# A CIN recommender tower: chunk 1's stores moved to SyncE's queue ahead of the layer-1 loads, and one more layer-2 group split late

## The chip, the cores and the metric

One core of one Trainium2 chip. The metric is device time in microseconds, from launch to end, of one execution; lower is better. Comparisons between kernels are of executions on the same chip.

## The reference

512 samples, 39 fields, embeddings of 16 numbers. Three layers of pairwise products (a compressed interaction network) and a small dense top, all in fp32:

```python
e = stack([tbl_f[ids[:, f]] for f in range(39)], axis=1)   # 512 x 39 x 16
x0 = xk = e
for idx, (W, b) in enumerate(params):                       # three layers, 128 outputs each
    z = relu(einsum('bhd,bkd,hks->bsd', x0, xk, W) + b)
    xk, direct_part = z[:, :64], z[:, 64:]                  # last layer: all of z is direct
logit = sum(concat(direct), axis=-1)                        # over d
h = relu(concat([logit, dense_ctx]) @ W_top1 + b_top1)
h = relu(h @ W_top2 + b_top2)
y = h @ W_top3
```

## The kernel before

The batch goes in NCH = 16 chunks of 32 samples; a chunk is N = 512 columns (sample, d). Layer 0 (L0) has 4 groups of products, layers 1 and 2 (L1, L2) have 10 each. A group is one VectorE multiplication (`prod`, 128x1024) whose two 512-column tiles TensorE then multiplies by weights and adds up in a PSUM bank `z`.

A group is summed in one of two ways. Whole: two fp32 matmuls, which the profile shows as four records. Split: ScalarE rounds the product to fp32r (`high`), GpSimd subtracts to get the rest (`low`), and TensorE runs six fp32r matmuls: high by high weights, high by low weights, low by high weights. `SPLIT` lists the split groups; four of them, in `THROUGH_PSUM`, go tile by tile through the bank `base`, with VectorE making the low half. `high` and `low` have HRING = 4 slots, `prod` has RING = 8.

`stages_of(i)` writes out the order: in step i come L0 of chunk i, the first 6 groups of L2 of chunk i-1 (4 in step 15), L1 of chunk i, the rest of L2 of chunk i-1. Every engine walks that list in order and waits on semaphores. The splits, the slots and the numbers waited for are all counted from it.

The inputs of a chunk: GpSimd gathers 10 tiles of table rows (`gat`, chunks 0 and 1 at the start); two copies of them are stored in DRAM (`x0_rows`, 2 x 1191 rows of 64 bytes, in four DMAs); one DRAM-to-DRAM DMA repeats them five times; then come `x0base` (three DMAs of 78 KB), `spread0` (the L0 factor, 1792 KB) and `spread` in three pieces (the L1 and L2 factor: 768, 768 and 1024 KB, groups 0 to 2, 3 to 5, 6 to 9). SyncE's queue issues all that, except in the start-up, where ScalarE issues some: the second copy of chunk 0, and for chunk 1 all stores (`store_x0(1, (0, 1))`), the repeat (`repeat_second`), and `x0base` and `spread0` (`load_second`). On ScalarE the stores and the repeat of chunk 1 stand after L0 of chunk 0 and before `shared_copies(0, x1, z0, ...)`, the relu copies that make the L1 factor `x1`; `load_second` stands behind those.

SyncE's queue at the start runs: weights, store and loads of chunk 0, `repeat_x0(0)`, the three L1 pieces of chunk 0, those of chunk 1, `store_x0(2)`, then the loop for the chunks after that. What is stored, repeated and loaded is the same in every chunk; in the start-up only the issuing queue and the order differ.

Of the kernel before, what the change touches and what calls it, by code (L numbers as in the profile page):

```python
# [8 lines left out]
P = 128  # L9
B = 512  # L10
F = 39
D = 16
S = 128
# [5 lines left out]
N = CB * D  # L19
# [24 lines left out]
RELU0_AFTER = (3, 3, 3)  # L44
PIECES = ((0, 3), (3, 6), (6, 10))
SPLIT = {"L0": (1,), "L2": (0, 1, 2, 5, 6, 8), "L1": (1, 2, 3, 5, 6, 7, 9)}
THROUGH_PSUM = (("L2", 2), ("L1", 2), ("L1", 6), ("L2", 6))
BASE_AFTER = ("L2", 9)
FIRST_GATHERS = {("L0", 1): 7, ("L1", 2): 1, ("L1", 5): 1, ("L1", 9): 1}
# [28 lines left out]
    return out  # L78

def finish_order(kind, gs):

    out = []
    for g in gs:
        if g not in SPLIT[kind]:
            out.append(g)
        if g - 1 in gs and g - 1 in SPLIT[kind]:
            out.append(g - 1)
    if gs[-1] in SPLIT[kind]:
        out.append(gs[-1])  # L90
    return out

# [4 lines left out]
DONE = {x: n + 1 for n, x in enumerate((c, kind, g) for c, kind, gs in STAGES for g in finish_order(kind, gs))}  # L97
SPLITS = [x for x in ORDER if x[2] in SPLIT[x[1]]]
# [39 lines left out]
def whole(kind):  # L138
    return [g for g in range(G1) if g not in SPLIT[kind]]

# [9 lines left out]
def tower_kernel(nc, ids, offsets, table, w0a, w0b, w1, w1_split, w2, w2_split, biases, wt1, bt1, wt2, bt2, wt3, ctxT, out):  # L150
    with ExitStack() as ctx:
        def sb(name, shape, dt=F32):
            return ctx.enter_context(nc.sbuf_tensor(name, shape, dt))
# [19 lines left out]
        high_w = {k: sb(f"high_w_{k}", [P, 2 * len(SPLIT[k]), S], F32R) for k in SPLIT}  # L173
        low_w = {k: sb(f"low_w_{k}", [P, 2 * len(SPLIT[k]), S], F32R) for k in SPLIT}
# [34 lines left out]
        h2_sum = (base, x2[:, 0, :])  # L209
        ctx_sum = (x1[:, 0, :], x1[:, 1, :], x2[:, 0, :], x2[:, 1, :])  # L210
        y_sum = (z0[0:1, 0:B // 2], z1[0:1, 0:B // 2])

        def sum_bank(c, kind):
            return z0 if kind == "L2" and c == NCH - 1 else {"L0": z0, "L1": z1, "L2": z2}[kind]
# [47 lines left out]
        def _(sp):  # L262
# [78 lines left out]
            for n, (at, end) in enumerate(FIRST_CUTS):  # L341
                load_first(at, end, spread0_first[n], (0, 1))
            repeat_x0(0)
            for p in range(len(PIECES)):
                load_spread(0, p)
            for p in range(len(PIECES)):
                load_spread(1, p)
            store_x0(2)
# [57 lines left out]

        @block.scalar
        def _(act):
            def split_weights(kind, rows, w):
                act.activation(high_w[kind][0:rows, :, :].rearrange("p t s -> p (t s)"), w, ACT.Copy  # L410
                               ).then_inc(high_w_ready, 1)

            def store_x0(c, copies):

                act.wait_ge(gathered[c], 16 * GAT)
                for n in copies:
                    first = x0_dram[c, n * F:n * F + 1, 0:1]
                    act.dma_start(bass.AP(first.tensor, first.offset, [[D, P], [FPT * N, GAT - 1], [1, D]]),
                                  gat[:, c, 0:GAT - 1, :]).then_inc(x0_stored[c], 16)
                    at = n * F + FPT * (GAT - 1)  # L420
                    tail = x0_dram[c, at:at + 1, 0:1]
                    act.dma_start(bass.AP(tail.tensor, tail.offset, [[D, LAST], [1, D]]),
                                  gat[0:LAST, c, GAT - 1, :]).then_inc(x0_stored[c], 16)

            def repeat_second():

# [7 lines left out]
            def load_second():  # L434

                for j in range(DPT):
                    row = x0_dram[1, (F - j * T0) % F:(F - j * T0) % F + 1, 0:1]
                    act.dma_start(x0base[j * F:(j + 1) * F, :], bass.AP(row.tensor, row.offset, [[N, F], [1, N]])
                                  ).then_inc(base_in, 16)
                act.wait_ge(prod_done, PROD_NUMBER[0, "L0", G0 - 1])  # L440
                act.wait_ge(x0_copied[1], 16)
                row = x0_dram[1, 0:1, 0:1]
                act.dma_start(spread0[:, :, :].rearrange("p t n -> p (t n)"),
                              bass.AP(row.tensor, row.offset, [[N, P], [1, T0 * N]])).then_inc(spread0_in, 16)

            def load_first():

# [101 lines left out]
            split_weights("L1", P, w1_part)  # L549
            act.wait_ge(w2_in, 32)  # L550
            split_weights("L2", P, w2_part)
            act.wait_ge(bias_in, 16)
            store_x0(0, (1,))
            load_first()
            take_base(0)
            for i in range(NCH + 1):
                if i == NCH:
                    shared_copies(i - 1, x2, z1, "L1", 1, x2_ready)
                    relu1(i - 1, 2)
                elif i >= 2:  # L560
                    for part in range(3):
                        relu1(i - 1, part)
                for c, kind, gs in stages_of(i):
                    for g in gs:
                        if (c, kind, g) in POOL_NUMBER:
                            take_high(c, kind, g)
                        if (c, kind, g) in TILED_NUMBER:
                            take_tile_high(c, kind, g, 0)
                        if tiled_behind(c, kind, g, 1):
                            take_tile_high(*tiled_behind(c, kind, g, 1), 1)  # L570
                        if i == 1 and kind == "L0" and g == 1:
                            shared_copies(0, x2, z1, "L1", 1, x2_ready)
                            relu1(0, 2)
                        if kind == "L0" and g == G0 - 1 and i >= 2:
                            relu2(i - 2)
                        if i == NCH and g == 2:
                            relu2(i - 2)
                        if kind == "L2" and i < NCH:
                            for part in range(3):
                                if g == RELU0_AFTER[part]:  # L580
                                    relu0(i, part)
                        if (kind, g) == BASE_AFTER and i + 1 < NCH and i >= 1:
                            take_base(i + 1)
                        if i == 0 and (kind, g) == ("L1", G1 - 1):
                            take_base(1)
                    if kind == "L0" and i == 0:
                        store_x0(1, (0, 1))
                        repeat_second()
                        shared_copies(0, x1, z0, "L0", 0, x1_ready)
                        relu0(i, 2)  # L590
                        load_second()
            relu2(NCH - 1)

            act.wait_ge(top_in, 16 * 4)
# [12 lines left out]
        def _(dve):  # L607
# [91 lines left out]
            def split_weights(kind, rows, w, done):  # L699

                dve.wait_ge(high_w_ready, done)
                dve.tensor_tensor(low_w[kind][0:rows, :, :].rearrange("p t s -> p (t s)"), w,
                                  high_w[kind][0:rows, :, :].rearrange("p t s -> p (t s)").bitcast(F32),
                                  ALU.subtract).then_inc(low_w_ready, 1)

            dve.wait_ge(w0_in, 32)
# [7 lines left out]
            dve.wait_ge(gathered[0], 16 * GAT)  # L714
            split_weights("L1", P, w1_part, 2)
            split_weights("L2", P, w2_part, 3)
            for i in range(NCH + 1):
                if i == NCH:
                    shared_copies(i - 1, x2, z1, "L1", 1, x2_ready)
# [28 lines left out]
        def _(pe):  # L748
# [11 lines left out]
            def sum_high(c, kind, g):  # L760

                z = sum_bank(c, kind)
                at = 2 * SPLIT[kind].index(g)
# [12 lines left out]
            def sum_low(c, kind, g, closes):  # L776

                z = sum_bank(c, kind)
                at = 2 * SPLIT[kind].index(g)
# [12 lines left out]
            def sum_stage(c, kind, gs):  # L792

                closing = stage_end(c, kind)
                if kind == "L2" and c == NCH - 1 and gs[0] == 0:
                    pe.wait_ge(r0_ready, NCH)
                elif gs[0] == 0 and c >= 1:
                    pe.wait_ge({"L0": r0_ready, "L1": r1_ready, "L2": r2_ready}[kind], c)
                for g in gs:
                    if g in SPLIT[kind]:  # L800
# [3 lines left out]
                    if g - 1 in gs and g - 1 in SPLIT[kind]:  # L804
                        sum_low(c, kind, g - 1, DONE[c, kind, g - 1] == closing)
                if gs[-1] in SPLIT[kind]:
                    sum_low(c, kind, gs[-1], DONE[c, kind, gs[-1]] == closing)

            pe.wait_ge(ctx_in, 16 * 3)
# [2 lines left out]
                          start=True, stop=True).then_inc(ctx_done, 1)  # L812
            pe.wait_ge(w1_in, 32)
            pe.wait_ge(w2_in, 32)
            pe.wait_ge(low_w_ready, 3)
            for i in range(NCH):
                for c, kind, gs in stages_of(i):
                    sum_stage(c, kind, gs)
# [95 lines left out]
```

## Time and profile before

| | |
|---|---|
| median of 3 runs | 661.51 us (660.06, 661.51, 1059.06) |
| the profiled execution | 660.79 us |
| its span, first to last instruction | 658.8 us |
| TensorE busy | 610.5 us (93%) |
| VectorE busy | 558.9 us (85%) |
| GpSimd busy | 536.6 us (81%) |
| ScalarE busy | 408.2 us (62%) |
| bytes moved | 90.29 MB, mean 137 GB/s |
| mean granted TensorE clock | 0.987 of full |

About 2 us lie outside the span. Of the three runs one is a far outlier; the other two and the profiled one lie within 1.5 us.

### The profile page before, as it was taken

The numbers are of one execution on the slowest core, as the hardware profiler recorded it, in microseconds if no ns is written. First come the engines' busy times: TensorE is split into PE (matmuls) and PEld (weight loads), VectorE is DVE, ScalarE is ACT, GpSimd is POOL, SyncE is SP. The second block draws the span as 40 slices with busy tenths as digits, with TensorE's granted clock in tenths as the row PEclk, the third lists the DMA queues.
The fourth block names the chain that finished last, engine by engine and source line by source line (L and its number), as shares of the span: only waits on it lengthen the run. The fifth ranks groups of instructions, "written<-read, shape, count | busy, mean of one in ns | idle before, by whom it ended". The sixth has DMA issues, their size and how long they took to land. (4 is left out here: it accounts for less than half of the span.)

```text
span 658.8 us, 6297 instructions
## 1 busy us (share of the span) xinstructions
PE 610.5 (93%) x2000; PEld 375.5 (57%) x2000; DVE 558.9 (85%) x632; ACT 408.2 (62%) x550; POOL 536.6 (81%) x325
## 2 busy tenths in 40 slices
PE   4137989999999999999999999999999999999998
PEld 1014546666666665666656665656666566665553
DVE  2327889898989989898989899898989898988971
ACT  2005576667585867766675857676676758575632
POOL 6755889898989989898989999898989896865540
PEclk9976999999999999999999999999999999999999
DMA  6678473655556584736464564737364645620000
GB/s 224 155 173 253 109 210 67 187 120 136 143 122 203 139 250 76 240 77 206 96 182 101 138 187 90 235 77 237 78 200 96 180 110 128 193 64 1 0 0 0
DMA packets 64043, 90.29 MB, mean 137 GB/s; under 512 B 46624, under 2 KB 49568, under 8 KB 60042
## 3 DMA queue, kind: packets, MB, share of 16 engines
q1 hardware_dynamic: 54334, 85.25, 47.1%
q0 software_dynamic: 5120, 1.29, 2.1%
q10 hardware_dynamic: 4556, 3.35, 1.8%
q8 instruction: 15, 0.25, 0.2%
q14 instruction: 18, 0.15, 0.1%
HBM read 87.31 MB, written 8.95 MB: 146 GB/s over the span
## 5 line engine op out<-in xcount | busy, mean ns | idle before, releaser
L385 POOL TENSOR_TENSOR low<-prod,high 128x1024 fp32r<-128x1024 f32 (+1 forms) x160 | 381.0, 2399 | 63.1 <-ACT high L474 60.3
L648 DVE TENSOR_TENSOR prod<-spread,x 128x1024 f32<-128x1024 f32 x256 | 308.1, 1214 | 42.1 <-issue 15.8
L756 PE MATMUL z<-prod,w_sb 128*128 128x512 f32 (+2 forms) x608 | 290.7, 598 | 30.3 <-DVE prod L648 15.4
L474 ACT ACTIVATE high<-prod 128x1024 fp32r<-128x1024 f32 (+1 forms) x160 | 167.9, 1058 | 119.6 <-DVE prod L648 98.0
L773 PE MATMUL z<-high,high_w_L 128*128 128x512 f32 (+1 forms) x448 | 203.0, 453 | 4.4 <-ACT high L484 2.6
L788 PE MATMUL z<-low,high_w_L 128*128 128x512 f32 (+1 forms) x448 | 181.9, 487 | 3.9 <-POOL low L385 2.4
L375 POOL DMA_INDIRECT gat<-table_dram,index x160 | 154.9, 968 | 36.5 <-issue 34.2
L756 PEld LDWEIGHTS z<-prod,w_sb 128*128 128x128 f32 (+2 forms) x608 | 115.8, 191 | 117.0 <-issue 86.6
L773 PE MATMUL z<-high,low_w_L 128*128 128x512 f32 (+1 forms) x448 | 177.9, 397 | 0.0
L788 PEld LDWEIGHTS z<-low,high_w_L 128*128 128x128 f32 (+1 forms) x448 | 82.1, 189 | 69.8 <-issue 45.7
L494 ACT ACTIVATE x<-z,bias_sb 64x512 f32<-64x512 f32 (+1 forms) x174 | 112.5, 646 | 14.0 <-PE z L756 7.4
L484 ACT ACTIVATE high<-base 128x512 fp32r<-128x512 f32 x128 | 75.5, 590 | 56.1 <-DVE base L688 55.6
L773 PEld LDWEIGHTS z<-high,high_w_L 128*128 128x128 f32 (+1 forms) x448 | 84.8, 189 | 42.4 <-issue 14.5
L773 PEld LDWEIGHTS z<-high,low_w_L 128*128 128x128 f32 (+1 forms) x448 | 84.8, 189 | 31.7 <-issue 14.4
L696 DVE TENSOR_TENSOR low<-base,high 128x512 fp32r<-128x512 f32 x128 | 87.8, 686 | 8.6 <-ACT high L484 8.3
L688 DVE TENSOR_TENSOR base<-spread,x 128x512 f32<-128x512 f32 x128 | 88.6, 692 | 2.3
L629 DVE TENSOR_TENSOR prod<-spread,base 117x1024 f32<-117x1024 f32 x64 | 65.4, 1082 | 10.6 <-DMA spread<-x_rows 6.9
L507 ACT ACTIVATE x<-z,bias_sb 32x512 f32<-32x512 f32 x12 | 7.7, 642 | 17.7 <-DMA x_rows<-gat 16.7
L544 ACT ACTIVATE r<-z,bias_sb 128x512 f32<-128x512 f32 x16 | 11.0, 687 | 10.5 <-PE z L788 10.4
L465 ACT ACTIVATE base<-x0base 117x512 f32<-117x512 f32 x16 | 9.6, 602 | 8.8 <-DMA x0base<-x_rows 8.4
L674 DVE TENSOR_REDUCE logit<-r 128x32 f32<-128x512 f32 x16 | 10.9, 678 | 4.8 <-ACT r L544 4.8
L811 PE MATMUL x<-ctx_sb,wt1c_sb 16*128 16x512 f32 x8 | 7.2, 1076 | 7.8 <-DMA bt_sb<-bt_dram 7.8
(37 smaller groups left out, 89.2 us busy)
## 6 DMA issues: line engine op xcount, KB each, us to landing
spread<-x_rows SPq DMA_DIRECT2D x14, 1792.0 KB
spread<-x_rows SPq DMA_DIRECT2D x32, 768.0 KB, 13.3
spread<-x_rows SPq DMA_DIRECT2D x16, 1024.0 KB
x_rows<-x_rows SPq DMA_DIRECT2D x15, 390.0 KB
x0base<-x_rows SPq DMA_DIRECT2D x44, 78.0 KB
gat<-table_dram,index POOLq DMA_INDIRECT x160
x_rows<-gat SPq DMA_DIRECT2D x29, 72.0 KB
spread<-x_rows ACTq DMA_DIRECT2D x1, 1792.0 KB
```

The source lines that it names most:

```text
L375: pool.indirect_dma_start(out=gat[0:rows, c % GBUF, j, :], out_offset=None, in_=table, in_offset=bass.IndirectOffsetOnAxis(ap=index[0:rows ...
L385: pool.tensor_tensor(low[0:rows, h, 0:k, :], prod[0:rows, slot(c, kind, g), 0:k, :], high[0:rows, h, 0:k, :].bitcast(F32), ALU.subtract).t ...
L474: act.activation(high[0:rows, split_slot(c, kind, g), 0:k, :], prod[0:rows, slot(c, kind, g), 0:k, :], ACT.Copy).then_inc(high_ready, 1)
L484: act.activation(high[0:rows, split_slot(c, kind, g), t, :], base[0:rows, :], ACT.Copy).then_inc(tile_high, 1)
L494: act.activation(to[at:end, tile, :], z[k:k + end - at, :], ACT.Relu, bias=bias_sb[k:k + end - at, layer:layer + 1]).then_inc(ready, 1)
L629: dve.tensor_tensor(prod[0:rows, slot(c, "L0", g), 0:k, :], spread0[0:rows, 2 * g:2 * g + k, :], base[0:rows, :].unsqueeze(1).to_broadcast ...
L648: dve.tensor_tensor(prod[0:rows, slot(c, kind, g), :, :], spread[0:rows, c % 2, g, :].unsqueeze(1).to_broadcast([rows, k, N]), x[0:rows, : ...
L688: dve.tensor_tensor(base[0:rows, :], spread[0:rows, c % 2, g, :], x[0:rows, t, :], ALU.mult).then_inc(tile_prod, 1)
L696: dve.tensor_tensor(low[0:rows, h, t, :], base[0:rows, :], high[0:rows, h, t, :].bitcast(F32), ALU.subtract).then_inc(tile_low, 1)
L756: last = pe.matmul(z[:, :], w[0:rows, at + j, :], prod[0:rows, slot(c, kind, g), j, :], start=g == 0 and j == 0, stop=closes and j == k - 1)
L773: pe.matmul(z[:, :], v[kind][0:rows, at + j, :], high[0:rows, h, j, :], start=g == 0 and j == 0 and v is high_w, stop=False)
L788: last = pe.matmul(z[:, :], high_w[kind][0:rows, at + j, :], low[0:rows, h, j, :], start=False, stop=closes and j == k - 1)
```

## The change

`store_again` is the second copy of chunk 0, two DMAs, as before. Start-up: chunk 1's four stores go from ScalarE's queue to SyncE's, right behind `repeat_x0(0)` and ahead of chunk 0's three L1 pieces. Chunk 1's `x0base` and `spread0` loads also go to SyncE's queue, between chunk 0's L1 pieces and chunk 1's. The repeat stays on ScalarE's queue, but now stands behind the relu copies, not ahead of them. Steady state: in the last three chunks group 7 of L2 is split (it was whole); its weights are split once at the start, by one more ScalarE and one more VectorE instruction of 128x256.

```diff
+LATE_SPLIT = {"L0": (), "L2": (7,), "L1": ()}
+LATE_FROM = {"L0": NCH, "L2": NCH - 3, "L1": NCH}
+def split_of(c, kind):
+    return tuple(sorted(SPLIT[kind] + (LATE_SPLIT[kind] if c >= LATE_FROM[kind] else ())))
...
@@ SyncE
             repeat_x0(0)
+            store_x0(1)
             for p in range(len(PIECES)):
                 load_spread(0, p)
+            load_base(1)
+            load_spread0(1)
             for p in range(len(PIECES)):
                 load_spread(1, p)
...
@@ ScalarE
-            def store_x0(c, copies):
+            def store_again():
+                act.wait_ge(gathered[0], 16 * GAT)
...
             split_weights("L2", P, w2_part)
+            split_weights("L2", P, late_part("L2", w2_sb), True)
             act.wait_ge(bias_in, 16)
-            store_x0(0, (1,))
+            store_again()
...
                     if kind == "L0" and i == 0:
-                        store_x0(1, (0, 1))
-                        repeat_second()
                         shared_copies(0, x1, z0, "L0", 0, x1_ready)
                         relu0(i, 2)
-                        load_second()
+                        repeat_second()
...
@@ VectorE
             split_weights("L2", P, w2_part, 3)
+            split_weights("L2", P, late_part("L2", w2_sb), 4, True)
...
@@ TensorE
-            pe.wait_ge(low_w_ready, 3)
+            pe.wait_ge(low_w_ready, 4)
```

`load_base(1)` waits for chunk 1's stores and for `base_ready` 1; `load_spread0(1)` waits for chunk 0's last L0 product and for the repeat; each piece of chunk 1 waits for the repeat.

## Rows read from the trace of the kernel before

**Rows 1.** Windows: busy time of each engine in a stretch of the steady state, clock, DMA share, GB/s
```profile
120.00:160.00 40.00, 39.87 (x138) 25.43 (x137) 35.56 (x41) 28.65 (x40) 36.23 (x24) 1.00 0.54 145
```
**Rows 2.** Timeline of VectorE in the first 70 us: start, duration, instruction, idle before
```profile
38.74 3.13 DVE L662 TENSOR_SCALAR x<-z,bias_sb 32x512 f32<-32x512 f32 x4 [4.42 <-PE z L756]
52.79 2.35 DVE L648 TENSOR_TENSOR prod<-spread,x 128x1024 f32<-128x1024 f32 x2 [10.92 <-ACT x L507]
...
64.15 1.22 DVE L648 TENSOR_TENSOR prod<-spread,x 128x1024 f32<-128x1024 f32 x1
...
68.84 4.08 DVE L629 TENSOR_TENSOR prod<-spread,base 117x1024 f32<-117x1024 f32 x4 [1.75 <-ACT base L465]
```
**Rows 3.** Waits: who waited for whom, us, times, longest
```profile
ACT x L507 <- DMA x_rows<-gat: 16.7, 1, 16.7
```
**Rows 4.** Timeline of ScalarE and of the DMAs it issues (ACTq)
```profile
34.05 0.39 ACTq L418 DMA_DIRECT2D x_rows<-gat  x1
...
36.05 6.22 ACTq L422 DMA_DIRECT2D x_rows<-gat  x1
49.16 0.90 ACTq L430 DMA_DIRECT2D x_rows<-x_rows  x1
50.11 0.64 ACT L507 ACTIVATE x<-z,bias_sb 32x512 f32<-32x512 f32 x1 [16.75 <-DMA x_rows<-gat]
50.25 0.83 ACTq L438 DMA_DIRECT2D x0base<-x_rows  x2
...
53.14 0.37 ACTq L443 DMA_DIRECT2D spread<-x_rows  x1
```
**Rows 5.** Timeline of all engines: VectorE's weight splits, and gathers on GpSimd
```profile
17.89 3.69 DVE L702 TENSOR_TENSOR low_w_L<-spread,high_w_L 128x1792 fp32r<-128x1792 f32 x2 [2.10 <-DMA gat<-table_dram,index]
17.95 2.79 POOL L375 DMA_INDIRECT gat<-table_dram,index  x1 [0.30 <-issue]
...
30.22 0.92 POOL L375 DMA_INDIRECT gat<-table_dram,index  x1 [0.30 <-issue]
```
**Rows 6.** Timeline: SyncE's DMA issues (SPq), and the ScalarE copy that waited for one
```profile
21.47 0.74 SPq L293 DMA_DIRECT2D x0base<-x_rows  x2
...
24.12 0.60 ACT L465 ACTIVATE base<-x0base 117x512 f32<-117x512 f32 x1 [8.42 <-DMA x0base<-x_rows]
...
25.41 0.92 SPq L282 DMA_DIRECT2D x_rows<-x_rows  x1
...
33.69 21.32 SPq L324 DMA_DIRECT2D spread<-x_rows  x6
...
81.43 0.36 SPq L308 DMA_DIRECT2D spread<-x_rows  x1
...
115.22 0.39 SPq L271 DMA_DIRECT2D x_rows<-gat  x1
...
116.76 0.60 SPq L274 DMA_DIRECT2D x_rows<-gat  x1
120.55 0.83 SPq L282 DMA_DIRECT2D x_rows<-x_rows  x1
```
**Rows 7.** Windows of 2 us: engines as in rows 1, clock, DMA share, GB/s
```profile
42.00:44.00 2.00, 0.00 (x0) 0.00 (x0) 0.00 (x0) 0.00 (x0) 1.46 (x2) 0.59 1.08 232
...
84.00:86.00 2.00, 2.00 (x7) 0.99 (x6) 1.10 (x1) 1.92 (x4) 1.39 (x3) 1.00 0.91 380
```
**Rows 8.** The chain that ended last: start, duration, what
```profile
629.77 1.72 PE z L756 x4
...
638.18 0.93 PE z L773 x4
```
**Rows 9.** The costliest groups: busy us, mean ns of one, idle before them
```profile
L385 POOL TENSOR_TENSOR low<-prod,high 128x1024 fp32r<-128x1024 f32 (+1 forms) x160 | 381.0, 2399 | 63.1 <-ACT high L474 60.3
```
**Rows 10.** Timeline of VectorE and TensorE in the last 65 us
```profile
595.43 1.22 DVE L648 TENSOR_TENSOR prod<-spread,x 128x1024 f32<-128x1024 f32 x1 [4.61 <-ACT x L494]
...
628.57 0.51 PE L773 MATMUL z<-high,high_w_L 128*128 128x512 f32 x1 [0.76 <-ACT high L484]
```

More of the change, by code:

```diff
@@ L78, in stages_of, with finish_order @@
     return out
-def finish_order(kind, gs):
+def split_of(c, kind):
+    return tuple(sorted(SPLIT[kind] + (LATE_SPLIT[kind] if c >= LATE_FROM[kind] else ())))
+def finish_order(c, kind, gs):
     out = []
+    split = split_of(c, kind)
     for g in gs:
-        if g not in SPLIT[kind]:
+        if g not in split:
             out.append(g)
-        if g - 1 in gs and g - 1 in SPLIT[kind]:
+        if g - 1 in gs and g - 1 in split:
             out.append(g - 1)
-    if gs[-1] in SPLIT[kind]:
+    if gs[-1] in split:
         out.append(gs[-1])
@@ L96 @@
 NUMBER = {x: n + 1 for n, x in enumerate(ORDER)}
-DONE = {x: n + 1 for n, x in enumerate((c, kind, g) for c, kind, gs in STAGES for g in finish_order(kind, gs))}
-SPLITS = [x for x in ORDER if x[2] in SPLIT[x[1]]]
+DONE = {x: n + 1 for n, x in enumerate((c, kind, g) for c, kind, gs in STAGES for g in finish_order(c, kind, gs))}
+SPLITS = [x for x in ORDER if x[2] in split_of(x[0], x[1])]
 SPLIT_NUMBER = {x: n + 1 for n, x in enumerate(SPLITS)}
@@ L172, in tower_kernel @@
         w2_sb = sb("w2_sb", [P, 2 * len(whole("L2")), S])
-        high_w = {k: sb(f"high_w_{k}", [P, 2 * len(SPLIT[k]), S], F32R) for k in SPLIT}
-        low_w = {k: sb(f"low_w_{k}", [P, 2 * len(SPLIT[k]), S], F32R) for k in SPLIT}
+        high_w = {k: sb(f"high_w_{k}", [P, 2 * len(SPLIT[k] + LATE_SPLIT[k]), S], F32R) for k in SPLIT}
+        low_w = {k: sb(f"low_w_{k}", [P, 2 * len(SPLIT[k] + LATE_SPLIT[k]), S], F32R) for k in SPLIT}
         wide1, wide2 = 2 * len(SPLIT["L1"]) * S, 2 * len(SPLIT["L2"]) * S
@@ L211, in tower_kernel, with split_weight_tiles, late_part @@
         y_sum = (z0[0:1, 0:B // 2], z1[0:1, 0:B // 2])
+        def split_weight_tiles(kind, late):
+            n = 2 * len(SPLIT[kind])
+            return (n, n + 2 * len(LATE_SPLIT[kind])) if late else (0, n)
+        def late_part(kind, w):
+            at = 2 * whole(kind).index(LATE_SPLIT[kind][0])
+            return w[:, at:at + 2, :].rearrange("p t s -> p (t s)")
         def sum_bank(c, kind):
@@ L408, in _, with split_weights @@
         def _(act):
-            def split_weights(kind, rows, w):
-                act.activation(high_w[kind][0:rows, :, :].rearrange("p t s -> p (t s)"), w, ACT.Copy
+            def split_weights(kind, rows, w, late=False):
+                at, end = split_weight_tiles(kind, late)
+                act.activation(high_w[kind][0:rows, at:end, :].rearrange("p t s -> p (t s)"), w, ACT.Copy
                                ).then_inc(high_w_ready, 1)
-            def store_x0(c, copies):
[L415 to L423, printed above, removed]
+            def store_again():
+                act.wait_ge(gathered[0], 16 * GAT)
+                first = x0_dram[0, F:F + 1, 0:1]
+                act.dma_start(bass.AP(first.tensor, first.offset, [[D, P], [FPT * N, GAT - 1], [1, D]]),
+                              gat[:, 0, 0:GAT - 1, :]).then_inc(x0_stored[0], 16)
+                tail = x0_dram[0, F + FPT * (GAT - 1):F + FPT * (GAT - 1) + 1, 0:1]
+                act.dma_start(bass.AP(tail.tensor, tail.offset, [[D, LAST], [1, D]]),
+                              gat[0:LAST, 0, GAT - 1, :]).then_inc(x0_stored[0], 16)
             def repeat_second():
@@ L432, in repeat_second @@
                               ).then_inc(x0_copied[1], 16)
[L434 to L444, printed above, removed]
             def load_first():
@@ L697, in take_tile_low, with split_weights @@
                                   ALU.subtract).then_inc(tile_low, 1)
-            def split_weights(kind, rows, w, done):
+            def split_weights(kind, rows, w, done, late=False):
+                at, end = split_weight_tiles(kind, late)
                 dve.wait_ge(high_w_ready, done)
-                dve.tensor_tensor(low_w[kind][0:rows, :, :].rearrange("p t s -> p (t s)"), w,
-                                  high_w[kind][0:rows, :, :].rearrange("p t s -> p (t s)").bitcast(F32),
+                dve.tensor_tensor(low_w[kind][0:rows, at:end, :].rearrange("p t s -> p (t s)"), w,
+                                  high_w[kind][0:rows, at:end, :].rearrange("p t s -> p (t s)").bitcast(F32),
                                   ALU.subtract).then_inc(low_w_ready, 1)
@@ L778, in sum_low @@
                 z = sum_bank(c, kind)
-                at = 2 * SPLIT[kind].index(g)
+                at = 2 * (SPLIT[kind] + LATE_SPLIT[kind]).index(g)
                 rows, k = shape_of(kind, g)
@@ L799, in sum_stage @@
                 for g in gs:
-                    if g in SPLIT[kind]:
+                    if g in split_of(c, kind):
                         sum_high(c, kind, g)
@@ L803, in sum_stage @@
                         sum_whole(c, kind, g, DONE[c, kind, g] == closing)
-                    if g - 1 in gs and g - 1 in SPLIT[kind]:
+                    if g - 1 in gs and g - 1 in split_of(c, kind):
                         sum_low(c, kind, g - 1, DONE[c, kind, g - 1] == closing)
-                if gs[-1] in SPLIT[kind]:
+                if gs[-1] in split_of(c, kind):
                     sum_low(c, kind, gs[-1], DONE[c, kind, gs[-1]] == closing)
```

2 lines of the change are left out of this document (1 added, 1 removed).

## The prediction

> **What bounds the kernel now.** I read the busy time by stretches first. From about 100 us on TensorE is busy without a gap (39.87 of 40 us, VectorE 35.6, GpSimd 36.2) [rows 1]: only less TensorE work, or an earlier start of this phase, moves the end. The start-up is different. VectorE finishes its four relu copies of chunk 0 at 41.87 (38.74 + 3.13), then idles 10.92 us until the first L1 product at 52.79, and the release is named: ScalarE's half of the same copies [rows 2]. The waits say why ScalarE is late: one wait of 16.7 us for chunk 1's stores [rows 3]. The timeline of ScalarE's queue shows the whole story: it issues the stores at 34.05, one issue takes 6.22 us, the stores have landed at 49.16, and only after the repeat is issued do the copies run from 50.11 [rows 4]. The copies need nothing of chunk 1; it is queue order alone. Meanwhile the DMA engines are full with chunk 0's L1 pieces, which SyncE issued from 33.69 on (2.6 MB, at 232 GB/s in the middle) [rows 6, 7].
>
> From the first L1 product the chain is VectorE's own: L1 takes from 52.79, with group 6 reached at about 64.15, to L0 of chunk 1 at 68.84, 16.05 us later [rows 2]. Whatever the first L1 product gains is kept as long as each load arrives in time for the earlier clock.
>
> **The start-up, part by part.**
>
> ScalarE's copies lose their cover of waits. They start with VectorE's, when L0's last matmul is done (38.7), and take 4 x 0.64 = 2.6 us [rows 2, 4]: done at 41.3. VectorE's, at 41.9, are then the later half. So the copies allow L1 at 41.9.
>
> What is late next is the first L1 piece, since SyncE's queue now issues four stores ahead of it. When can those go? The first store on ScalarE's queue went at 34.05 [rows 4], 2.9 us after the last gather of chunk 1 was issued (30.22 + 0.92) [rows 5]; ScalarE's queue runs ahead of its arithmetic (at 50.25 it issues a load while four activations are still to come [rows 4]), so I take 34.05 as the gathers' landing. One store sequence on SyncE's queue takes 2.14 us to issue (115.22 to 116.76 + 0.60) and 5.33 us until the repeat behind it may go (120.55) [rows 6]. So the first piece is issued at 36.2 instead of 33.69, and the stores have landed at 39.4. The piece is 786 KB: at 232 GB/s 3.4 us, and a small load takes 1.9 us from issue to use (22.21 to 24.12) [rows 6, 7]; 5.3 us, and with the stores' rest in front of it on the same engines up to 6.2. It lands between 41.5 and 42.4. The two terms are near each other; I take 42.2.
>
> One small term on top. VectorE gets one more subtraction of 128x256 right behind the two of 3.69 us. In their shadow a gather took 2.79 us instead of 0.92 [rows 5], so the blocks go together. At 3.69 us for 3328 columns, 256 more are 0.3 to 0.4 us; chunk 1's gathers end that much later, and with them the stores and the piece. The bounds are 0 and 0.4; I take 0.3, because the gather's row shows the effect directly. The Trainium skill ("SBUF — State Buffer", Who interferes with whom) speaks the other way: it infers that tensor_tensor takes only the pair's read side, which does not hold up a gather's descriptors. By that the term would be 0 and the sum 0.3 us better; the row of 2.79 us decides. The same instruction on ScalarE and the raised wait of TensorE (4 instead of 3) end by about 22 us, ahead of the base copy at 24.12 on which every L0 product waits [rows 6]: nothing.
>
> First L1 product: 42.5, against 52.79. Gain 10.3 us. Bounds: 41.9 (gain 10.9) and, if the store issues are as slow as the 6.22 us one, 34.05 + 8.2 + 6.2 = 48.4 (gain 4.4).
>
> Does the rest follow? Group 6 needs the third piece at 42.5 + 11.4 = 53.9. Three pieces of 2.62 MB at 232 GB/s take 11.3 us from about 38: 49.4, plus landing 50.4, plus a share for the repeat: in time. ScalarE issues the repeat now between 39.4 and 42.2, beside these loads. Alone it took 4.0 us (49.16 to 53.14) [rows 4]; chunk 0's, beside other loads, 8.3 (25.41 to 33.69) [rows 6]. So it lands between 43.4 and 50.5; I take 49, as nearest to the crowded row. The wait in front of it holds up ScalarE no longer: the stores (39.4) are in before the copies end. Then SyncE issues `spread0` of chunk 1: 1.84 MB at 380 GB/s are 4.8 us, plus 1.9 [rows 7, 6], with `x0base` ahead: 56 to 57. L0 of chunk 1 wants it at 42.5 + 16.05 = 58.5. It fits by 1.5 us, no more. Chunk 1's L1 pieces, behind it, are in by 69, and wanted at about 76. Cost of these edits: nothing, under that cover; without it, us for us.
>
> TensorE's clock does not come back: it had fallen to 1.2 GHz by 42 to 44 (0.59 in that window) [rows 7], and the first L1 matmul now comes near 43.8, behind the fall. The slow stretch moves along, under VectorE's chain.
>
> **The late split.** A whole group costs TensorE 1.72 us (4 records), a split one six records at 0.93 / 4, 1.40 [rows 8]: 0.32 us less, three times 0.96. It counts only where TensorE sets the end. Chunk 13's (in step 14) does: VectorE later waits 4.61 us for the copies that hang on TensorE's L0 of chunk 15 [rows 10]. From there VectorE leads until TensorE waits last at 628.57 [rows 10]; chunk 14's saving falls in that stretch and is lost. Chunk 15's group 7 comes behind 628.57, on TensorE's chain: kept. So 0.64, upper bound 0.96. The cover: each new split adds a rounding on ScalarE (28.65 of 40 us busy [rows 1]) and a subtraction of 2.4 us on GpSimd [rows 9], which in those steps has no gathers left, ten of 0.92 us [rows 5]. If GpSimd were late all the same, with groups 5, 7 and 8 in a row, TensorE would wait up to 2.4 us once per chunk; on the two chunks that count this is 4.8 against 0.64, the lower bound of -4.2. TensorE takes the low half a group later than the high one, so I stay at 0.64.
>
> **Sum.** 660.8 - 10.3 - 0.6 = 649.9 us, span about 648. The profiled run is 0.7 us below the median of the runs; against that median it is -1.75%. About 2%, 13.2 us, is what a measurement of this kernel can tell from no change as I use the word.
>
> **The rivals.**
>
> Late `spread0`: the repeat crawls, landing at 51 to 54, and L0 of chunk 1 waits 0.5 to 3.5 us. For it: the margin is 1.5 us and the stores' crawl; against: the repeat has only 195 rows of 2 KB. Price 652 (650.5 to 653.5). Chance 0.16.
>
> Stuck issue: SyncE's store issues take what ScalarE's did, the first piece lands at 48.4: 660.8 - 4.4 - 0.6 = 655.8. For it: the one row of 6.22 us; against: SyncE's own row of 2.14. Chance 0.07.
>
> Slower: the pieces flow only when the stores are in, and the stores crawl as they did (15.1 us, to 49.2); the first piece then lands at 49.2 + 6.2 = 55.4, 2.6 us behind 52.79, and the time is 660.8 + 2.6 - 0.6 = 662.8. It decides from stores that land after 46.6. Against it: what made them crawl were the pieces, now behind them. Chance 0.03.
>
> More than the sum: all terms at their good ends (10.9 + 0.96) give 648.9. For the bound of 2% still another us would be needed, such as a first matmul ahead of the clock's fall, or a baseline at the high end of its runs. Chance 0.09, with 647 to 648.5. That the change doesn't do what it says (the split saves nothing) would be 650.5; that it costs its 4.2 us, 654.7; both lie inside the range, the second with a chance of 0.03 taken from the forecast's. The forecast itself, 648.9 to 651.5: 0.62.
>
> Range 647.7 to 655.0: it leaves out the slower case, the stuck issue and half of the best. Faster by over 2%: 0.12; same: 0.84; slower by over 2%: 0.04, for what I have not seen.
>
> **What the new profile would show.** ScalarE's 16.7 us wait gone, its copies beside VectorE's at 38.8; first L1 product at 42 to 43, with a short idle put down to the first piece if my second term holds; L0 of chunk 1 at 58 to 59 without a DMA wait; the phase without gaps about 10 us earlier; TensorE's last wait again on ScalarE in step 16; six records for group 7 in the last chunks. The forecast is wrong if the first product comes after 44, or if VectorE waits for `spread` or ScalarE for `x0base` at chunk 1.

## The result and the profile after

The changed kernel takes 652.12 us in the median of 4 runs (651.20 to 652.47), the kernel before 661.77 on the same chip (661.51 without its outlier of 1059.06 us, which the ratio leaves out): a ratio of 0.9861, 95% interval 0.9837 to 0.9884. The profiled execution took 651.20 us with a span of 649.4, against 660.79 and 658.8. The forecast was 649.9 in a range of 647.7 to 655.0, and "within 2%" was the likeliest class: both hold. The time is 1.3 us (profiled) to 2.2 us (median) above the forecast. The gain is 1.3 us short, 9.6 us against 10.9 us, between the medians as between the profiled executions, since the kernel before has its median above its profiled execution too.

The number alone would not have settled the cause. The median of 652.12 lies outside the 648.9 to 651.5 of "the forecast itself" and inside the 650.5 to 653.5 of the rival with a late `spread0`. The rows decide between the two.

The spans differ by 9.4 us. I follow them by four marks, each a row: first L1 product, first L0 product of chunk 1, first L1 product of chunk 1, TensorE's last wait. VectorE's timeline after, which answers to [rows 2] (78.18 is layer 1 of chunk 1; before it stood at 86.94):

```profile
38.52 3.13 DVE L666 TENSOR_SCALAR x<-z,bias_sb 32x512 f32<-32x512 f32 x4 [3.83 <-PE z L762]
43.70 2.35 DVE L652 TENSOR_TENSOR prod<-spread,x 128x1024 f32<-128x1024 f32 x2 [2.06 <-DMA spread<-x_rows]
...
47.01 1.22 DVE L652 TENSOR_TENSOR prod<-spread,x 128x1024 f32<-128x1024 f32 x1 [0.23 <-DMA spread<-x_rows]
...
60.08 4.08 DVE L633 TENSOR_TENSOR prod<-spread,base 117x1024 f32<-117x1024 f32 x4 [1.75 <-ACT base L470]
...
78.18 2.35 DVE L652 TENSOR_TENSOR prod<-spread,x 128x1024 f32<-128x1024 f32 x2 [1.84 <-ACT x L499]
```

The 10.92 us wait for ScalarE is gone, and a wait of 2.06 us for the first piece stands in its place; then 0.23 us for the second piece. The first L1 product comes 9.09 us earlier than in [rows 2], L0 of chunk 1 8.76 us earlier, layer 1 of chunk 1 8.76 us earlier.

ScalarE and its DMA issues (ACTq) after, against [rows 4]: the copies run beside VectorE's, and the repeat goes at 38.46, since the queue runs ahead of the arithmetic.

```profile
38.44 0.64 ACT L512 ACTIVATE x<-z,bias_sb 32x512 f32<-32x512 f32 x1 [5.26 <-PE z L762]
38.46 0.90 ACTq L447 DMA_DIRECT2D x_rows<-x_rows  x1
39.11 1.98 ACT L512 ACTIVATE x<-z,bias_sb 32x512 f32<-32x512 f32 x3
```

SyncE's issues (SPq) after, against [rows 6]:

```profile
34.57 0.39 SPq L286 DMA_DIRECT2D x_rows<-gat  x1
...
36.75 1.91 SPq L339 DMA_DIRECT2D spread<-x_rows  x3
38.78 1.41 SPq L308 DMA_DIRECT2D x0base<-x_rows  x3
51.77 0.35 SPq L323 DMA_DIRECT2D spread<-x_rows  x1
```

The four stores take 2.18 us of issue, the first piece goes at 36.75, and `spread0` of chunk 1 at 51.77, when the repeat has landed.

The chain that ended last, after, answers to [rows 8, 10]: TensorE waits last at 619.42 (628.57 before), and group 7 of chunk 15 is now in the run of eight records at 0.23 us each.

```profile
619.42 0.73 PE z L779 x2
...
625.94 1.86 PE z L779 x8
```

So: 9.09 at the first product, 0.33 lost by group 3's later start (3.31 us behind the first product instead of 2.99), 8.76 kept over chunk 1, 0.39 gained until the last wait (9.15), 0.25 behind it (649.4 - 619.42 = 29.98, before 658.8 - 628.57 = 30.23). Sum 9.4. The first two experiments ask how much of the 0.39 is the split's.

### The profile page after: what moved, and what is told of

Its sections match the earlier page's. It is cut to its first block and busy times, and to the rows that moved or that the text cites. A ratio compares the mean times of both kernels' runs of the same rounds, so it can differ in the third digit from the quotient of the medians.

```text
span 649.4 us, 6321 instructions
## 1 busy us (share of the span) xinstructions
PE 607.9 (94%) x2006; PEld 375.3 (58%) x2006; DVE 559.2 (86%) x633; ACT 411.6 (63%) x554; POOL 543.3 (84%) x328
## 5 line engine op out<-in xcount | busy, mean ns | idle before, releaser
L403 POOL TENSOR_TENSOR low<-prod,high 128x1024 fp32r<-128x1024 f32 (+1 forms) x163 | 388.0, 2398 | 47.3 <-ACT high L479 46.0
L762 PE MATMUL z<-prod,w_sb 128*128 128x512 f32 (+2 forms) x596 | 284.6, 598 | 22.1 <-DVE prod L633 15.5
L479 ACT ACTIVATE high<-prod 128x1024 fp32r<-128x1024 f32 (+1 forms) x163 | 171.1, 1058 | 123.4 <-DVE prod L652 102.9
L393 POOL DMA_INDIRECT gat<-table_dram,index x160 | 154.6, 966 | 36.5 <-issue 33.8
L762 PEld LDWEIGHTS z<-prod,w_sb 128*128 128x128 f32 (+2 forms) x596 | 113.3, 190 | 107.0 <-issue 85.8
L489 ACT ACTIVATE high<-base 128x512 fp32r<-128x512 f32 x128 | 75.5, 590 | 51.7 <-DVE base L692 51.2
L666 DVE TENSOR_SCALAR x<-z,bias_sb 32x512 f32<-32x512 f32 x12 | 9.1, 757 | 4.2 <-PE z L762 3.8
```

The lines of the kernel that those rows point to most:

```text
L393: pool.indirect_dma_start(out=gat[0:rows, c % GBUF, j, :], out_offset=None, in_=table, in_offset=bass.IndirectOffsetOnAxis(ap=index[0:rows ...
L403: pool.tensor_tensor(low[0:rows, h, 0:k, :], prod[0:rows, slot(c, kind, g), 0:k, :], high[0:rows, h, 0:k, :].bitcast(F32), ALU.subtract).t ...
L479: act.activation(high[0:rows, split_slot(c, kind, g), 0:k, :], prod[0:rows, slot(c, kind, g), 0:k, :], ACT.Copy).then_inc(high_ready, 1)
L489: act.activation(high[0:rows, split_slot(c, kind, g), t, :], base[0:rows, :], ACT.Copy).then_inc(tile_high, 1)
L762: last = pe.matmul(z[:, :], w[0:rows, at + j, :], prod[0:rows, slot(c, kind, g), j, :], start=g == 0 and j == 0, stop=closes and j == k - 1)
```

## The experiments

Each is told by the same marks. Unless a diff says otherwise, it is against the changed kernel.

**Without the late split.**

```diff
-LATE_FROM = {"L0": NCH, "L2": NCH - 3, "L1": NCH}
+LATE_FROM = {"L0": NCH, "L2": NCH, "L1": NCH}
```

> The changed kernel without the late split (group 7 of layer 2 whole in all chunks; its extra weight split at the start is kept). My theory: the split gave 0.3 us ahead of TensorE's last wait (chunk 13) and 0.3 us behind it (chunk 15), nothing for chunk 14; so this kernel's span is 0.6 us above the changed kernel's, 650.0, about 651.9 us; first L1 product still at 43.7. Rival (all three chunks count): 1.0 us. Rival (the split is absorbed): 0.0 us.

Measured: 652.45 us in the median (651.52 to 654.61), the profiled one 651.52, span 649.7. Its last wait is in the chain at

```profile
619.46 0.74 PE z L779 x2
```

From there to the end 30.24 us, against 29.98 with the split: chunk 15's 0.3 us. At the first L1 product, at layer 1 of chunk 1 and at that wait the two profiles agree within 0.05 us. Chunk 13's share is there all the same, between ScalarE's last two sets of six relu copies: they start at 570.71 and 582.31 without the split, and at 570.96 and 582.26 with it, 11.60 against 11.30 us. The 490 us before took 0.24 us more in the profile with the split, and this hides the share in the total; what caused it is open. This pair alone does not settle 0.3 or 0.6.

**The late split alone, on the start-up of before.** Every start-up edit of the diff is taken back, the split is kept.

> The kernel before with the late split alone (the start-up as before: stores, repeat, x0base and spread0 of chunk 1 on ScalarE's queue). Theory: 0.3 us from chunk 13 (the step from ScalarE's second-to-last layer-1 input copies to its last ones shrinks from 11.6 to 11.3 us) and 0.3 us behind TensorE's last wait: 660.1 us, a ratio of 0.999. Rival: nothing, 660.8 us, with that step still 11.6.

Measured over 10 runs: 660.61 us, ratio 0.9990, interval 0.9980 to 0.9999. Layer 1 of chunk 1 on VectorE, and TensorE's last wait:

```profile
86.18 2.35 DVE L674 TENSOR_TENSOR prod<-spread,x 128x1024 f32<-128x1024 f32 x2 [1.84 <-ACT x L519]
```

```profile
627.50 0.50 PE L801 MATMUL z<-high,high_w_L 128*128 128x512 f32 x1 [0.76 <-ACT high L509]
```

541.32 us lie between them; before it was 628.57 - 86.94 = 541.63. Another 30.0 us to the end, 30.2 before. That is 0.3 and 0.2, the two shares of the forecast. The difference of the medians, 0.67 us, agrees, but its interval (0.1 to 1.3 us) would also hold 0.96, all three chunks. ScalarE's last two sets of six relu copies say where the 0.3 arises, first before, then with the split alone:

```profile
579.79 4.00 ACT L494 ACTIVATE x<-z,bias_sb 64x512 f32<-64x512 f32 x6
591.40 4.00 ACT L494 ACTIVATE x<-z,bias_sb 64x512 f32<-64x512 f32 x6 [0.53 <-PE z L756]
```

```profile
579.05 4.00 ACT L519 ACTIVATE x<-z,bias_sb 64x512 f32<-64x512 f32 x6
590.35 4.00 ACT L519 ACTIVATE x<-z,bias_sb 64x512 f32<-64x512 f32 x6 [0.33 <-PE z L784]
```

11.61 us before, 11.30 with the split: chunk 13's share, as in the pair above. From the last set to TensorE's last wait it takes 37.17 us before, 37.15 with the split alone, 37.15 in the changed kernel without the split and 37.16 with it: chunk 14's saving is lost.

**The repeat ahead of ScalarE's copies.**

```diff
+                        repeat_second()
                         shared_copies(0, x1, z0, "L0", 0, x1_ready)
                         relu0(i, 2)
-                        repeat_second()
```

> The changed kernel, but ScalarE waits for the stores and issues the repeat ahead of its relu copies, as before the change. Theory (the gain is the stores on SyncE's queue, ahead of the pieces: they land at 38.2, before L0 ends at 38.5): no change, within 0.3 us of the changed kernel, the repeat issued at about 38.2. Rival (the gain is the order on ScalarE): the copies come late again and several us are lost.

Measured: 651.93 us (651.65 to 652.61). ScalarE, then VectorE:

```profile
37.93 0.90 ACTq L447 DMA_DIRECT2D x_rows<-x_rows  x1
38.89 2.65 ACT L512 ACTIVATE x<-z,bias_sb 32x512 f32<-32x512 f32 x4 [5.62 <-DMA x_rows<-gat]
```

```profile
43.23 2.35 DVE L652 TENSOR_TENSOR prod<-spread,x 128x1024 f32<-128x1024 f32 x2 [2.22 <-DMA spread<-x_rows]
...
59.30 4.08 DVE L633 TENSOR_TENSOR prod<-spread,base 117x1024 f32<-117x1024 f32 x4 [1.75 <-ACT base L470]
```

ScalarE again waits for the stores, but they are in at 37.93, when L0 ends, and nothing is lost. With the stores on SyncE's queue ahead of the pieces the place of the repeat on ScalarE's decides nothing.

**The stores behind the copies on ScalarE's queue.**

```diff
@@ SyncE
-            store_x0(1)
@@ ScalarE
                         relu0(i, 2)
+                        store_second()
                         repeat_second()
```

> The changed kernel, but the four stores stay on ScalarE's queue, behind the relu copies; SyncE loads the pieces of chunk 0 at once. Theory: the copies are done at 41.3 and the first L1 product starts at 41.9, earlier than in the changed kernel, but the stores crawl beside the pieces to about 50, ScalarE stands in the wait of the repeat till then, and VectorE is stopped at the first tile of group 2 (from about 45 to 50); the repeat lands at 54, spread0 of chunk 1 at about 61, L0 of chunk 1 starts at 61 to 63 instead of 60.1: 652.5 to 654.5 us. Rival (order on ScalarE alone makes the gain): 649 to 650 us.

Measured: 656.81 us, ratio 0.9928 (0.9907 to 0.9949). ScalarE, then VectorE:

```profile
43.23 4.78 ACTq L449 DMA_DIRECT2D x_rows<-gat  x1
49.94 0.89 ACTq L457 DMA_DIRECT2D x_rows<-x_rows  x1
50.88 1.06 ACT L489 ACTIVATE high<-prod 128x1024 fp32r<-128x1024 f32 x1 [9.09 <-DMA x_rows<-gat]
```

```profile
41.66 2.35 DVE L663 TENSOR_TENSOR prod<-spread,x 128x1024 f32<-128x1024 f32 x2
...
52.59 0.69 DVE L711 TENSOR_TENSOR low<-base,high 128x512 fp32r<-128x512 f32 x1 [6.73 <-ACT high L499]
...
64.53 4.08 DVE L644 TENSOR_TENSOR prod<-spread,base 117x1024 f32<-117x1024 f32 x4 [1.75 <-ACT base L480]
```

The chain is the one expected: an early start, slow stores (38.44 to 49.94), ScalarE in the wait, VectorE stopped 6.73 us at group 2. So the order on ScalarE's queue alone also gives the early first product. The size was missed: L0 of chunk 1 at 64.5, not 61 to 63, and 656.8 us, not 652.5 to 654.5, since I had not counted the work that group 2's roundings still have ahead of them when ScalarE comes free. The profiled execution also has the fall of the clock that is told further below; it costs 1.2 us behind these rows. The order without the move keeps about half of the gain (0.9928 against 0.9861).

**`x0base` and `spread0` of chunk 1 on ScalarE's queue.**

```diff
@@ SyncE
-            load_base(1)
-            load_spread0(1)
@@ ScalarE
                         repeat_second()
+                        load_second()
```

> The changed kernel with chunk 1's x0base and spread0 loads back on ScalarE's queue, behind the repeat. Theory: ScalarE stands in the wait for the repeat until about 51.7, VectorE is stopped at group 2 of layer 1 (about 46.5 to 53), and L0 of chunk 1 starts at about 65 instead of 60.1: 655 to 657 us. Rival (ScalarE's issues run ahead and block nothing): within 0.5 us of 651.2.

Measured: 656.94 us, ratio 0.9928 (0.9907 to 0.9949). ScalarE, then VectorE:

```profile
52.58 1.06 ACT L489 ACTIVATE high<-prod 128x1024 fp32r<-128x1024 f32 x1 [11.43 <-DMA x_rows<-x_rows]
```

```profile
54.29 0.69 DVE L711 TENSOR_TENSOR low<-base,high 128x512 fp32r<-128x512 f32 x1 [5.53 <-ACT high L499]
...
66.22 4.08 DVE L644 TENSOR_TENSOR prod<-spread,base 117x1024 f32<-117x1024 f32 x4 [1.75 <-ACT base L480]
```

The chain is the one expected, with L0 of chunk 1 at 66.2 and not 65. Before the change this wait cost next to nothing: it was over at 53.14 [rows 4], and ScalarE's next rounding, at 55.18, waited for VectorE's product. With layer 1 started early it costs 4.8 us (656.94 against 652.12): this edit carries as much as the move of the stores.

**The first piece ahead of the stores.**

```diff
             repeat_x0(0)
+            load_spread(0, 0)
             store_x0(1)
-            for p in range(len(PIECES)):
+            for p in range(1, len(PIECES)):
                 load_spread(0, p)
```

> The changed kernel with chunk 0's first L1 piece ahead of chunk 1's stores on SyncE's queue. Theory (the first product waits for that piece, and right behind it the second piece is the bound): the first product comes at about 41.7, 2 us earlier, but group 3 then waits for the second piece, which still lands at about 47; L0 of chunk 1 stays at 59.5 to 60.5, and the time within 0.6 us of the changed kernel's 651.2. Rival (the first piece alone is the bound): L0 of chunk 1 at 58, time 649.2.

Measured: 652.06 us (650.69 to 652.85). SyncE's issues, then VectorE:

```profile
34.30 0.60 SPq L339 DMA_DIRECT2D spread<-x_rows  x1
...
36.69 3.66 SPq L289 DMA_DIRECT2D x_rows<-gat  x1
40.39 1.19 SPq L339 DMA_DIRECT2D spread<-x_rows  x2
```

```profile
41.86 2.35 DVE L653 TENSOR_TENSOR prod<-spread,x 128x1024 f32<-128x1024 f32 x2
...
47.42 1.22 DVE L653 TENSOR_TENSOR prod<-spread,x 128x1024 f32<-128x1024 f32 x1 [2.49 <-DMA spread<-x_rows]
...
60.48 4.08 DVE L634 TENSOR_TENSOR prod<-spread,base 117x1024 f32<-117x1024 f32 x4 [1.75 <-ACT base L471]
```

The first product comes 1.84 us earlier and all of it is given back at group 3. The bound is not the first piece but the first two together. A store issued behind a piece here also held SyncE up: one issue took 3.66 us.

**The repeat held back until the first piece is in.**

```diff
                 act.wait_ge(x0_stored[1], 64)
+                act.wait_ge(spread_in[0][0], 16)
```

> The changed kernel with the repeat of chunk 1 held back until the first piece of chunk 0 has landed. Theory A (the piece needs 6.8 us from issue to landing because the repeat's packets share its engines): the first product comes at 42.5 to 43.0 instead of 43.7, but the repeat, 4 us later, lands at 53 or later and spread0 of chunk 1 at 60 to 61, so L0 of chunk 1 starts at 61 to 62 and the time is 652 to 653. Theory B (the piece's time is its own): first product still at 43.5 to 43.9, same end.

Measured: 652.18 us (651.67 to 652.92). ScalarE's issue of the repeat, then VectorE:

```profile
43.71 0.89 ACTq L448 DMA_DIRECT2D x_rows<-x_rows  x1
```

```profile
43.73 2.35 DVE L653 TENSOR_TENSOR prod<-spread,x 128x1024 f32<-128x1024 f32 x2 [2.16 <-DMA spread<-x_rows]
...
60.48 2.35 DVE L634 TENSOR_TENSOR prod<-spread,base 117x1024 f32<-117x1024 f32 x2 [1.75 <-ACT base L471]
```

Theory A falls: without the repeat beside it the first piece is as late. The repeat itself lost only 1 us by going 5.3 us later (`spread0` goes at 52.79, not 51.77). The packet records in the two traces show why: issued at 38.46 its first data packet starts at 45.08, 6.6 us later, and issued at 43.71 at 50.22, 6.5 us later. Its packets then take 5.9 us in the one and 2.1 in the other, where the third piece is in at 51.90. Alone, before the change, the first started 1.7 us behind the issue. L0 of chunk 1 still does not wait for a DMA.

**Group 5 of layer 2 whole for chunk 0.** In the changed kernel TensorE waits twice in step 1 for this one split group: ScalarE's rounding stands behind six relu copies, and GpSimd's subtraction behind that. TensorE's timeline there:

```profile
79.99 0.50 PE L779 MATMUL z<-high,high_w_L 128*128 128x512 f32 x1 [0.72 <-ACT high L479]
...
82.45 0.73 PE L794 MATMUL z<-low,high_w_L 128*128 128x512 f32 x2 [1.26 <-POOL low L403]
```

```diff
+EARLY_WHOLE = {"L0": (), "L2": (5,), "L1": ()}
...
     split = SPLIT[kind] + (LATE_SPLIT[kind] if c >= LATE_FROM[kind] else ())
-    return tuple(sorted(split))
+    return tuple(sorted(g for g in split if c > 0 or g not in EARLY_WHOLE[kind]))
...
-    return [g for g in range(G1) if g not in SPLIT[kind]]
+    return [g for g in range(G1) if g not in SPLIT[kind] or g in EARLY_WHOLE[kind]]
```

> The changed kernel with group 5 of layer 2 whole for chunk 0 only (its weights are loaded both ways). TensorE waits in step 1 for this group: 0.72 us for ScalarE's rounding, which stands behind six relu copies, and 1.26 us for GpSimd's subtraction, and it is never idle afterwards. Theory: the two waits go, the group costs 0.32 us more, and the phase without gaps starts up to 1.7 us earlier, of which VectorE's pace in layer 1 of chunk 1 takes some back: 649.5 to 650.5 us. The short fall of the granted clock near 82 us, which some runs of the changed kernel show and which costs 1.2 us, should be rarer. Rival (VectorE leads there, TensorE's lag is no loss): no change.

Measured: 650.61 us (650.13 to 651.16), ratio 0.9834 (0.9817 to 0.9851), 0.1 us above the expected range. Both waits are gone; TensorE has none between these two, of which the first stands in the changed kernel too:

```profile
74.53 0.50 PE L781 MATMUL z<-high,high_w_L 128*128 128x512 f32 x1 [0.76 <-ACT high L491]
84.73 0.51 PE L781 MATMUL z<-high,high_w_L 128*128 128x512 f32 x1 [0.27 <-ACT high L491]
```

From layer 1 of chunk 1 (78.53) to the last wait (619.15) it is 540.62 us instead of 541.24. Small waits of 0.2 to 0.6 us for ScalarE and GpSimd appear in layer 1, 1.1 us in all: they took back two thirds of the 1.7 us. That VectorE's pace is behind them, as I expected, is not shown.

**Groups 0, 1 and 5 whole for chunk 0, and both others again on the same chip.**

The diff is against the kernel with group 5 alone.

```diff
-EARLY_WHOLE = {"L0": (), "L2": (5,), "L1": ()}
+EARLY_WHOLE = {"L0": (), "L2": (0, 1, 5), "L1": ()}
```

> The changed kernel with groups 0, 1 and 5 of layer 2 whole for chunk 0 (weights loaded both ways), not group 5 alone. TensorE idled 1.35 us in step 1 for ScalarE's rounding of group 0. Theory: that stretch follows VectorE, so groups 0 and 1 bring nothing for the end, but TensorE is busier there and the granted clock does not fall near 82 us in any run: 650.1 to 650.8 us, within 0.4 us of the kernel with group 5 alone. Rival (0.64 us more TensorE work counts): 651.2 us.

> The changed kernel once more, beside the two variants on the same chip. Expected: runs in two groups, about 651.2 to 651.8 us without a fall of the granted clock near 82 us and about 652.5 us with one (mean clock lower), median near 652.

> The kernel with group 5 of layer 2 whole for chunk 0 once more, on the same chip as the changed kernel. Expected: 650.2 to 651.0 us, 1.2 to 1.6 us below the changed kernel's median; if the first comparison was only the chip, the same as the changed kernel.

Measured, five runs each: groups 0, 1 and 5 whole 650.52 us (649.55 to 650.88), ratio to before 0.9826 (0.9811 to 0.9841); group 5 alone 650.96 (650.41 to 651.57), 0.9835 (0.9820 to 0.9849); the changed kernel 652.01 (651.01 to 654.12), 0.9859 (0.9839 to 0.9878). So each variant's median lies 1.0 to 1.5 us below the changed kernel's, twice for group 5, while the intervals of the ratios overlap at their ends. Groups 0 and 1 bring nothing clear on top (0.4 us), as expected. The expected two groups of runs did not come out: the changed kernel's five runs have mean granted clocks of 0.992 and 0.995, but the fastest (651.01) has 0.992 and a slower one (652.01) has 0.995.

The changed kernel's two profiled executions show something else that sets its times apart. The windows of 4 us of the one that took 651.20 us and of the one that took 651.88 (columns as in [rows 1]; the seventh figure, after the five busy times, is the granted clock):

```profile
82.00:86.00 4.00, 3.55 (x12) 2.28 (x13) 3.94 (x6) 1.90 (x3) 3.85 (x4) 1.00 0.97 334
```

```profile
82.00:86.00 4.00, 4.00 (x8) 1.97 (x8) 3.97 (x6) 1.36 (x3) 3.84 (x3) 0.59 1.01 329
```

In the second TensorE runs at 1.2 GHz for most of that stretch and does 8 matmul records where the other does 12. VectorE is then held up a few us later:

```profile
88.85 0.69 DVE L700 TENSOR_TENSOR low<-base,high 128x512 fp32r<-128x512 f32 x1 [1.34 <-ACT high L489]
```

That execution started layer 1 of chunk 1 at 77.41, 0.77 us ahead of the other, and had its last wait at 620.00, 0.58 behind: 1.35 us lost in between, 1.26 of it by ScalarE's six copies near 110 us (at 110.47 and 110.96). The profiles with the repeat ahead, the stores behind (there at 86 to 90 us), the piece first and the repeat held back have the same fall, and 542.5 us between those marks (from 77.38, 82.61, 78.57 and 78.57 to 619.89, 625.07, 621.09 and 621.09); those without the fall (the changed kernel, without the late split, the split alone, the loads on ScalarE) have 541.2 to 541.4.

## Why the prediction was right, and by how much not

**What bounds the kernel.** Right. The 16.7 us wait was a matter of queue order: either cure alone lets the first L1 product start early, the copies ahead of the stores (41.66) or the stores ahead of the pieces (43.23). What was won reached the end: 8.76 us at layer 1 of chunk 1 and 9.15 at the last wait. Of the 0.4 us by which the second is larger, 0.3 are chunk 13's share. (In the profile without the split the last wait still comes 9.11 us earlier: there the 490 us up to the last steps are 0.3 us shorter than before, and why is open.)

**When the copies are done.** Predicted 41.9; VectorE's end at 38.52 + 3.13 = 41.65.

**The first piece, the term that was mis-sized.** Predicted 42.5, measured 43.70: 1.2 us of the 1.5 missing in the span (9.4 us against 10.9; 0.2 us outside the span came back). The issue was nearly right (36.5 against 36.75), in part by luck: the 36.5 holds 0.3 us for the subtraction, which cost nothing, while the first store went 0.5 us later than the 34.05 of [rows 4]. From issue to use the piece took 6.95 us, not 6.0. I had built it from a rate and the latency of a load of 78 KB, with 5.3 and 6.2 as ends, and the true value lies outside. The repeat is not to blame: it was held back, and nothing came sooner.

The packet records and semaphore events in the traces say what the sum lacked. The piece's first packet starts 1.4 us behind the issue. Its 16 closing packets, of four bytes each, end on average 3.5 us behind that, much as 3.4 us from the mean rate has it, but the last of them ends 4.6 us behind, and VectorE waits for the last: the 16 semaphore events come between 41.78 and 43.61, the product at 43.70. The 1.9 us of latency, too, was counted from the end of an issue and used from its start. The stores explain little. Their packets end at 37.46, ahead of the piece's first at 38.16. With no store in front, a piece took 6.2 us from issue to its last event (piece first, 34.30 to 40.53) and 6.7 (stores behind the copies, 33.50 to 40.23), against 6.9 here and 6.7 to 7.4 in all nine profiles with stores in front. So the term was too short without them as well, and whether the rest is theirs stays open. The high end of the range covered it.

**The one more subtraction.** Predicted 0.3 us of delay to the gathers. Measured: GpSimd and VectorE after,

```profile
18.10 2.74 POOL L393 DMA_INDIRECT gat<-table_dram,index  x1 [0.30 <-issue]
21.15 1.36 POOL L393 DMA_INDIRECT gat<-table_dram,index  x1 [0.30 <-issue]
...
30.31 0.92 POOL L393 DMA_INDIRECT gat<-table_dram,index  x1 [0.30 <-issue]
```

```profile
21.61 0.42 DVE L707 TENSOR_TENSOR low_w_L<-w_sb,high_w_L 128x256 fp32r<-128x256 f32 x1
```

The last gather is issued 0.09 us later than in [rows 5], and that offset is there before the subtraction (18.10 against 17.95). The gather beside it took 1.36 us, as before without it. The term is 0. The Trainium skill ("SBUF — State Buffer", Who interferes with whom) infers that a tensor_tensor does not hold up a gather's descriptors; I had set that aside, and for this instruction it was right. It does not explain the gather of 2.74 us beside the two subtractions of 3.69 us together. In twelve of the thirteen profiles that gather took 2.5 to 2.8 us. In the one with groups 0, 1 and 5 whole it took 0.94 us beside the same subtractions and the next one 1.63, so the last gather was issued at 28.99, 1.3 us earlier. The first store still went at 34.13: a shift of the gathers' issue does not carry over to the stores one for one, as the sum had it.

**Does the rest follow.** The step had a wrong label and a hole. What I called group 6 at +11.4 us is group 8; group 6's first tile stands at +8.3, which by my own figures is 50.8 against a third piece in at 50.4. It was in time: the piece's last event is at 51.40, and the tile starts at 52.34. And I never priced the second piece, which is wanted at +3.0: it cost 0.33 us here, and it is what the piece-first kernel ran into. The repeat landed at about 51.7, not 49, as late as the rival with a late `spread0` had it (51 to 54); yet L0 of chunk 1 never waited for a DMA. In the kernel with the held-back repeat `spread0` was issued another 1.0 us later, and L0 still did not wait. So that rival's condition came true and its price did not. `spread0` was in at 58.91, 7.2 us behind the repeat, within the 7 to 8 us I had given it, and L0 itself came 1.6 us later (60.08, not 58.5), which left 1.2 us. That the late first piece moved L0 back is luck for this step.

**The clock.** Wrong, without cost: I wrote that the slow stretch would move along. It shrank. The granted clock was 0.53 over 42 to 60 us before and 0.51 over 41 to 48 after:

```profile
42.00:60.00 18.00, 5.93 (x11) 3.39 (x12) 7.14 (x9) 6.57 (x9) 5.41 (x5) 0.53 0.78 223
```

```profile
41.00:48.00 7.00, 3.02 (x5) 1.48 (x5) 4.67 (x5) 2.43 (x4) 3.42 (x4) 0.51 1.03 253
```

VectorE sets the pace there: from its first L1 product to L0 of chunk 1 it took 16.05 us before and 16.38 after, and the 0.33 between them is the second piece's.

**The late split.** Right in place, and nearly in size: 0.3 and 0.2 us at the two places that count, measured with the split alone, against 0.32 each, and nothing for chunk 14. The lower bound of -4.2 us was not needed.

**The slower rival.** Stores that crawl were made once more (on ScalarE's queue, beside the pieces), and cost 4.7 us of the gain, not all of it. Behind the pieces' start they took 11.5 us (38.44 to 49.94); ahead of them, on SyncE's queue, they were in 3.6 us after the first issue (34.29 to 37.93 in the kernel with the repeat ahead). The stuck issue did not come either: 2.18 us.

**The signs.** Of those listed, the first product at 42 to 43 and L0 of chunk 1 at 58 to 59 were missed (43.70 and 60.08); the first stood 0.3 us short of the 44 past which the forecast would have been wrong. The others came: no 16.7 us wait, a short idle put down to the first piece, no DMA wait at chunk 1, the last wait on ScalarE.

**The median.** 0.9 us of the difference to 652.12 is not in the profiled execution at all: other executions of the same kernel run up to 1.3 us longer, in the second set of five up to 2.9. The fall of the clock near 82 us goes with 1.3 us in one profile; what makes the rest is open. The "-1.75%" sets a forecast for the profiled execution against the median of the kernel before; like against like 10.9 us are 1.65%, and 1.4% was measured.

## What to carry to other kernels

A queue that issues DMAs and also computes should never hold a wait for data that its next computation doesn't need; but look at both sides of the move: undoing the move of the stores or that of the two loads took back over 4 us each of 9, while the place of the repeat was worth nothing. When a wait is removed, price every transfer that the earlier start will ask for, the second piece as well as the first. A split that pays where an engine is the bound can cost where that engine starves: choose it by the step, not by the kernel.

## What the runs showed of the hardware

The granted TensorE clock can fall again in the middle of work, in one execution and not in the next of the same kernel. In 68 to 82 us of the changed kernel TensorE was busy 10.2 of 14 us and kept its clock; with the repeat held back it was busy 10.6 and lost it behind 82 us. With group 5 whole, three profiled executions show no fall near 82 us; whether the missing waits are the reason stays open.

A DRAM-to-DRAM repeat of 390 KB beside 2.6 MB of loads on the other queue landed at 51.7 us when issued at 38.46 and at 52.7 when issued at 43.71, with its first data packet 6.6 and 6.5 us behind the issue. Issued when the pieces were in (49.94, stores behind the copies), it landed at 54.0.

The 16 completion events of one load of 768 KB spread over 1.8 us (41.78 to 43.61), so bytes over mean rate gave too short a time for its last one.
